# A graph attention whose aggregation products are issued in four parts between the K turns, one quad later

## The reference

```python
scores = jnp.einsum('ehd,ehd->eh', q[tgt], k[srcidx])        # 8 heads of 64
m = jax.ops.segment_max(scores, tgt, num_segments=n)
p = jnp.exp(scores - m[tgt])
s = jax.ops.segment_sum(p, tgt, num_segments=n)
w = p / (s[tgt] + 1e-16)
agg = jax.ops.segment_sum(w[:, :, None] * v[srcidx], tgt, num_segments=n)
```

## Time and profile before

| | us |
|---|---|
| median of 3 runs | 3487.64 (3484.23 to 3498.01) |
| the profiled execution | 3486.91 |
| its span | 3485.6 |
| PE busy | 2825.2 (81%) |
| POOL busy | 1161.3 (33%) |
| DVE, ACT busy | 1626.5, 1323.0 |
| attention of layer 0, steady part | 545 to 1380 of the span |
| attention of layer 1, steady part | 1960 to 2740 of the span |

### The profile page before, as it was taken

How to read it: one execution, slowest core, us unless ns; L and a number is a source line. 1 busy time by engine, 2 the same in 40 slices (tenths; PEclk the granted TensorE clock), 3 DMA queues, 4 the chain that set the end, 5 groups by cost and what they waited for, 6 DMA issues and landing times.

```text
span 3485.6 us, 78342 instructions
## 1 busy us (share of the span) xinstructions
PE 2825.2 (81%) x32605; PEld 2291.8 (66%) x32605; DVE 1626.5 (47%) x3272; ACT 1323.0 (38%) x3690; POOL 1161.3 (33%) x1130
## 2 busy tenths in 40 slices
PE   6999978888888888587996777777777758588888
PEld 5877866666676676464885666666666646366676
DVE  5247764444444444547123333333443455655443
ACT  3324434444444444322322344444444412243333
POOL 0000015555555555100012555655565401312110
PEclk8999989999999999789998899998988979799989
DMA  6531037887888888430234777777777642022211
GB/s 215 218 139 68 28 127 237 264 268 264 269 269 273 266 270 270 109 117 0 91 148 147 253 260 263 268 261 258 264 261 259 184 114 72 25 78 89 64 52 53
DMA packets 231795, 621.75 MB, mean 178 GB/s; under 512 B 39008, under 2 KB 45792, under 8 KB 231427
## 3 DMA queue, kind: packets, MB, share of 16 engines
q0 software_dynamic: 137088, 466.78, 40.1%
q1 hardware_dynamic: 94339, 149.78, 12.9%
HBM read 538.80 MB, written 103.39 MB: 184 GB/s over the span
## 4 chain that ended last, share of the span: by engine, by line
PE 75%; issue 12%; DVE 8%; DMA 2%; ACT 2%; another core or an unknown queue 1%; POOL 0%; SPq 0%; POOLq 0%; DVEq 0%; ACTq 0%
PE ps L1179 12%; PE ps L1221 9%; PE ps L1209 6%; PE ps L574 4%; PE ps L576 4%; PE ps L575 4%; PE ps L1186 3%; PE ps L774 3%; PE ps L942 2%; PE ps L944 2%; PE ps L943 2%; PE ps L1867 2%; PE ps L1171 1%; PE ps L1869 1%; PE ps L1868 1%
## 5 line engine op out<-in xcount | busy, mean ns | idle before, releaser
L1096 POOL DMA_INDIRECT Y<-KVd,srcE x449 | 457.2, 1018 | 374.9 <-PE ps L1221 237.8
L1277 DVE TENSOR_REDUCE stage<-ps 128x4 f32<-128x512 f32 x208 | 143.8, 692 | 629.8 <-remote 501.1
L1346 ACT ACTIVATE work<-ps 128x512 f32<-128x512 f32 x309 | 179.7, 597 | 506.8 <-PE ps L1179 472.3
L1221 PE MATMUL ps<-Y,G 128*32 128x64 f32 x7184 | 237.7, 226 | 161.9 <-issue 158.9
L1346 ACT ACTIVATE G<-ps 128x512 f32<-128x512 f32 x315 | 182.1, 598 | 421.8 <-PE ps L1179 388.4
L1096 POOL DMA_INDIRECT WA<-KVd,srcE x186 | 188.6, 1014 | 419.4 <-PE ps L576 266.3
L1221 PEld LDWEIGHTS ps<-Y,G 128*32 128x32 f32 x7184 | 181.9, 112 | 207.2 <-issue 202.7
L1365 ACT ACTIVATE stage<-ps,stage 128x128 f32<-128x128 f32 x832 | 294.0, 366 | 35.0 <-PE ps L1186 27.1
L1179 PE MATMUL ps<-ident,Y 128*128 128x128 f32 x1796 | 261.3, 303 | 2.6 <-issue 1.4
L574 PE MATMUL ps<-Wh,xs 128*128 128x512 f32 x600 | 239.0, 398 | 29.9 <-DVE xs L514 29.8
L1179 PEld LDWEIGHTS ps<-ident,Y 128*128 128x128 f32 x1796 | 231.9, 158 | 29.3 <-issue 21.0
(11 more groups left out here) (383 smaller groups left out, 6950.0 us busy)
## 6 DMA issues: line engine op xcount, KB each, us to landing
KVd<-stage SPq DMA_DIRECT2D x96, 256.0 KB, 2.0
aggd<-work SPq DMA_DIRECT2D x6, 2048.0 KB, 7.4
Qd<-stage SPq DMA_DIRECT2D x48, 256.0 KB, 2.0
G<-aggd SPq DMA_DIRECT2D x48, 256.0 KB, 2.7
Y<-KVd,srcE POOLq DMA_INDIRECT x449
Y<-in_x SPq DMA_DIRECT2D x4, 1536.0 KB, 15.0
G<-mixq SPq DMA_DIRECT2D x24, 256.0 KB
mixd<-rowsb SPq DMA_DIRECT2D x24, 256.0 KB
```

Source lines behind the costliest of these rows:

```text
L1096: pool.indirect_dma_start(out=kvs[a], out_offset=None, in_=KVd[l][:, :], in_offset=bass.IndirectOffsetOnAxis(ap=srcE[:, n:n + 1], axis=0)) ...
L1221: mm = pe.matmul(AG[32 * i:32 * i + 32, DH * h:DH * (h + 1)], probs[x][:, i, h, :], kvs[a][:, D + DH * h:D + DH * (h + 1)], start=(x == 0 ...
L1277: dve.tensor_reduce(smin[:, 4 * g:4 * g + 4], SC[g % 2][:, :].rearrange("p (c e) -> p c e", c=4), AXX, ALU.min).then_inc(mins, 1)
L1346: act.activation(kT[n % len(kT)], banks(l)[place_of(l, "k", n) % len(banks(l))][:, :], ACT.Copy).then_inc(out_a, 1)
```

## The change

Four things are altered.

1. In PE's round g the aggregation is that of quad g-3 (AGG_AT = 3), while the turn of the probabilities stays at quad g-2 (P_AT = 2).
2. `gather(g, i)` is one part: the eight products of tile i, all in column group i. Part 0 is issued after the second K turn of the round, parts 1 and 2 after the third and fourth, part 3 after the turn of the probabilities and ahead of the masks. The number of products is the same.
3. `agg` is raised once for each part, so by four in a quad; POOL's `fetch(n)` waits for the part of tile n-KV alone. All other waits on `agg` count by tiles.
4. In POOL's round the scatter stands ahead of the fetch of the queries. Because AGG_AT is odd now, both fall into the odd rounds; before, the scatter fell into even ones. On DVE the copy of the finished sums comes ahead of `least`. Each layer has one round more.

```diff
--- before.py
+++ after.py
@@ -27,7 +27,7 @@
 CAP = 16
 MASK = 2.0 ** 100
 LOOK = (2, 2)
-AGG_AT = 2
+P_AT, AGG_AT = 2, 3
 FAR = 8192.0
 BIG = 1.0e30
 EPS = 1e-5
@@ -835,8 +835,8 @@
                     order.append(("hot", b + 2))
                 if x == 1 and b + 1 < NJ:
                     order.append(("q", b + 1))
-                if g >= AGG_AT:
-                    order.append(("p", g - AGG_AT))
+                if 0 <= g - P_AT < NQ:
+                    order.append(("p", g - P_AT))
             place, by, count = {}, [], {"a": 0, "d": 0}
             for e, (kind, n) in enumerate(order):
                 who = "d" if kind in ("hot", "p") or kind == "k" and n % 4 == K_DVE[l] else "a"
@@ -1092,7 +1092,7 @@
             def fetch(n):
                 a = n % KV
                 if n >= KV:
-                    pool.wait_ge(agg, NQ * l + (n - KV) // 4 + 1)
+                    pool.wait_ge(agg, ET * l + n - KV + 1)
                 pool.indirect_dma_start(out=kvs[a], out_offset=None, in_=KVd[l][:, :],
                                         in_offset=bass.IndirectOffsetOnAxis(ap=srcE[:, n:n + 1], axis=0)
                                         ).then_inc(kv_in[a], 16)
@@ -1132,12 +1132,12 @@
                 fetch(n)
             at = KV
             for g in range(NQ + AGG_AT + 2):
+                x = (g - 2 - AGG_AT) // 2
+                if g % 2 == AGG_AT % 2 and 0 <= x < NJ:
+                    scatter(x)
                 j = (g + 3) // 2
                 if g % 2 and j < NJ:
                     fetch_slots(j)
-                x = (g - 2 - AGG_AT) // 2
-                if g % 2 == AGG_AT % 2 and 0 <= x < NJ:
-                    scatter(x)
                 while at < ET and (at - KV) // 4 <= g - AGG_AT:
                     fetch(at)
                     at += 1
@@ -1210,17 +1210,16 @@
                                    kT[n % len(kT)][:, k * P:(k + 1) * P], start=False, stop=True, skip_group_check=True)
                 mm.then_inc(sc, 1)
 
-            def gather(g):
-                x = g % 2
-                is_emptied(pe, l, place_of(l, "p", g))
-                if x == 0 and g:
-                    pe.wait_ge(ev, NJ * l + g // 2)
+            def gather(g, i):
+                x, a = g % 2, (4 * g + i) % KVN[l]
+                if i == 0:
+                    is_emptied(pe, l, place_of(l, "p", g))
+                    if x == 0 and g:
+                        pe.wait_ge(ev, NJ * l + g // 2)
                 for h in range(H):
-                    for i in range(4):
-                        a = (4 * g + i) % KVN[l]
-                        mm = pe.matmul(AG[32 * i:32 * i + 32, DH * h:DH * (h + 1)], probs[x][:, i, h, :],
-                                       kvs[a][:, D + DH * h:D + DH * (h + 1)], start=(x == 0 and h == 0), stop=(x == 1),
-                                       skip_group_check=True)
+                    mm = pe.matmul(AG[32 * i:32 * i + 32, DH * h:DH * (h + 1)], probs[x][:, i, h, :],
+                                   kvs[a][:, D + DH * h:D + DH * (h + 1)], start=(x == 0 and h == 0), stop=(x == 1),
+                                   skip_group_check=True)
                 mm.then_inc(agg, 1)
 
             if l == 0:
@@ -1239,21 +1238,23 @@
                 for i in range(4):
                     if 4 * g + LOOK[l] + i < ET:
                         turn_k(4 * g + LOOK[l] + i)
+                    if i >= 1 and g >= AGG_AT:
+                        gather(g - AGG_AT, i - 1)
                     if i == 1:
                         next(side, None)
                 if x == 0 and b + 2 < NJ:
                     turn_hot(b + 2)
                 if x == 1 and b + 1 < NJ:
                     turn_q(b + 1)
+                if 0 <= g - P_AT < NQ:
+                    turn_p(g - P_AT)
                 if g >= AGG_AT:
-                    turn_p(g - AGG_AT)
+                    gather(g - AGG_AT, 3)
                 next(side, None)
                 if g < NQ:
                     masks(g)
                     for i in range(4):
                         score(4 * g + i)
-                if g >= AGG_AT:
-                    gather(g - AGG_AT)
                 next(side, None)
 
         def attend_dve(l, side, begin, work_free):
@@ -1268,7 +1269,7 @@
                 x = g % 2
                 bank = bank_of("p", g)
                 if g >= 2:
-                    dve.wait_ge(agg, NQ * l + g - 1)
+                    dve.wait_ge(agg, ET * l + 4 * (g - 1))
                 dve.tensor_copy(probs[x][:, :, :, CAP * x:CAP * (x + 1)],
                                 bank[:, :].rearrange("p (c h s) -> p c h s", c=4, h=H)).then_inc(out_d, 1)
 
@@ -1291,7 +1292,7 @@
                 dve.tensor_tensor(p4, p4, rec4[:, :].unsqueeze(2).to_broadcast([P, 4, P]), ALU.mult).then_inc(normed, 1)
 
             def empty_agg(j):
-                dve.wait_ge(agg, NQ * l + 2 * j + 2)
+                dve.wait_ge(agg, ET * l + 4 * (2 * j + 2))
                 if j or l:
                     dve.wait_ge(sct, 16 * (NJ * l + j))
                 dve.tensor_copy(stage[:, 0, :], AG[:, :]).then_inc(ev, 1)
@@ -1321,15 +1322,15 @@
                 next(side, None)
                 if x == 0 and b + 2 < NJ:
                     empty_hot(l, b + 2)
-                if g >= AGG_AT:
-                    empty_p(g - AGG_AT)
+                if 0 <= g - P_AT < NQ:
+                    empty_p(g - P_AT)
                 next(side, None)
+                if g >= AGG_AT and (g - AGG_AT) % 2:
+                    empty_agg((g - AGG_AT) // 2)
                 if g < NQ:
                     least(g)
                 if 0 <= g - 1 < NQ:
                     normalise(g - 1)
-                if g >= AGG_AT and (g - AGG_AT) % 2:
-                    empty_agg((g - AGG_AT) // 2)
                 if x == 1 and b + 3 < NJ:
                     one_hot(l, b + 3)
                 next(side, None)
@@ -1387,7 +1388,7 @@
                 next(side, None)
 
         def edges_done(e, l):
-            e.wait_ge(agg, NQ * (l + 1))
+            e.wait_ge(agg, ET * (l + 1))
             e.wait_ge(ev, NJ * (l + 1))
 
         def edges_stored(e, l):
```

## The result

The changed kernel takes 4093.88 us (median of four runs, 4092.27 to 4096.43). The kernel before, beside it, takes 3492.82 (3484.23 to 3501.8). The ratio is 1.172, with a 95% interval of 1.169 to 1.176. That is 601 us more, where 367 were forecast; 4093.88 lies 4 us above the upper end of the range.

The account below looks back on a forecast made before the run. A ring between POOL's indirect-DMA chains and the PE stalls they cause was taken as the bound, with PE's work overtaking it after the change. Layer 1 +112, layer 0 +245 and extra rounds 10 made +367 on 3487: 3854 us, range 3530 to 4090.

Parts of the forecast that it names:

- The parts in series: Aggregation on PE: 16 matmuls of a part run in one column group, 0.88 us a part, 3.5 a quad against 0.9.
- Mode changes: PE between parts and full-array turns: ten changes a quad instead of two, 0.1 us each, +0.8 us, bounds 0 and 1.6.
- The stall: PE behind POOL's chain of five in odd rounds: 2.8 us a pair in layer 1, 2.3 in layer 0; even quads 0.5.
- The clock: PE's speed in both layers: the sum has no term for a lower clock; only rival C prices one.
- PE's own work: PE's time in a quad with no stall, after the change: 8.1 us in layer 1, 9.9 in layer 0.
- The sum's bases: Quad times of the kernel before, from which the additions are counted: 8.88 us in layer 0, 8.65 in layer 1.
- Moved waits: K turns waiting for K|V buffers held one round longer, layer 0: 0 to 1 us a pair, taken as 0.
- DVE's and the scatter's new places: DVE's copy of sums ahead of `least` and POOL's scatter ahead of the query fetch: both cost nothing.
- A: Rival, both layers: parts end the stalls, mode changes stay; +56 us, 3543; chance 0.18.
- D: Rival, both layers: POOL-PE ring broken, no stall left, mode changes hide; -133 us, 3354; chance 0.09.
- B: Rival, both layers: every round stalls in full, 2.3 us more in each even quad; +235 to the sum, 4089; chance 0.12.
- C: Rival, both layers: PE's clock falls to 1.2 GHz for half of the quads; +510 us, about 4360; chance 0.08.

Follow-up runs that it names:

- e1: Changed kernel with each of its four parts made of two heads of all four tiles, buffers released by quad: 3499.19 us, beside 3119.86 for the kernel before.
- e2: Kernel before, aggregation whole at its old place, with its tile loop outside the head loop: 3325.12 us, against 3119.86 unchanged.
- f1: Kernel before with K|V read by plain DMAs of SP (neighbouring rows) instead of POOL's indirect ones, chip with the stall: 3134.97 us against 3465.55.
- e6: Changed kernel with POOL's query fetch of odd rounds moved behind three K|V fetches, chip without the stall: 3608.38 us; kernel before 3137.59.
- r2: Changed kernel, unedited, on a chip without the stall: 3764.17 us against 3139.17 for the kernel before, ratio 1.200.

## Why the prediction was right in kind and too small

**The parts in series: right.** 55 ns a start and 0.88 us a part were forecast; 57 ns and 0.9 were measured. In layer 1, e1 against the kernel after shows that this order, and not the places, is the main cost. In layer 0 it isn't shown, since there the lateness holds e1 as well.

**Mode changes: right, a little small.** Of the pitch of 1.60 us, 16 x 57 ns = 0.91 and 4 x 109 ns = 0.44 are matmuls; 0.25 is left for two changes, 0.12 each, 0.1 in the forecast. e2 gives 0.12 as well. Without stalls and waits a quad is then 8.45 and 10.17 us, forecast 8.1 and 9.9: 0.35 and 0.27 too little, (0.35 + 0.27) x 102 = 63 us of the 234 missed.

**The stall: right in place and in size.** It stands where it was forecast, once in two rounds, behind the chain of five that starts at `turn_q`. In the even round its own fetches with their gaps cause none in the rows above. The pair of layer 1 that ran at the full clock throughout gives its size: 20.00 - 2 x 8.45 = 3.1 us, where 2.8 + 0.5 = 3.3 were forecast. Its first pause comes after some 50 matmuls and the idle that the profile lists after 59 (63 in the forecast), and it ends 1.16 us after the chain, not 0.3 to 0.9. f1 shows that the stall depends on the way in which K|V is fetched; that it is POOL's issuing stays an inference.

**The clock: the step that failed.** The sum counted PE's own work at 2.4 GHz throughout and had no term for what runs at 1.2 GHz behind a stall. Between 2505.13 and 2509.87 above PE takes 4.74 us for two parts and a K turn; at full clock these take 1.01 + 0.58 + 1.01 = 2.6. Not every pair loses as much: the three windows give 22.63 us at a mean clock of 0.85, 21.47 at 0.92, 20.00 at 1.00, and the mean of the layer, 21.8, lies 1.8 above the last. So the missing term is 1.8 us in a pair of layer 1. The forecast pair of 19.5, plus 0.7 of own work, less 0.2 of stall, plus 1.8 is the 21.8 measured.

The rows were there. The earlier trace rows shows turns at half speed behind a stall, and the earlier trace rows a mean of 0.90. I used them only for a rival that spread the lower clock over half of all quads. The mean clock of layer 1 is nearly the same before and after (0.89 in both windows above), so the low clock isn't new; what it costs is. Two neighbouring quads of the kernel before, from one chain of POOL to the next:

```profile
2310.12:2318.64 8.52, 5.97 (x126) 5.25 (x125) 2.84 (x6) 4.25 (x13) 5.12 (x5) 1.00 0.82 282
2318.64:2327.20 8.56, 7.14 (x123) 6.39 (x122) 3.95 (x9) 3.30 (x11) 5.11 (x6) 0.81 0.78 244
```

The second has its K turns at the lower clock and is only 0.04 us longer, because the turns ran beside POOL's chain, which set the length of a quad. In the changed kernel PE sets it, and every us lost to the clock counts.

In layer 0 a pair is 25.0 us, forecast 22.6. Of this 20.3 is PE's own (e6), so 4.7 are stall and lower clock together where 2.8 had been set. How they divide isn't measured. An estimate from the window's clock of 0.93: PE is at 1.2 GHz for 14% of 25.0 us, which costs at most half of that, 1.75, and leaves 3.0 or more for the stalls. The two layers' excess is (21.8 - 19.5)/2 x 102 = 117 and (25.0 - 22.6)/2 x 102 = 122. About 63 of it is own work, some 90 the clock in layer 1, and most of the rest, up to 89 by the estimate, the clock in layer 0. The sum's bases also differ by a few us from the later windows (8.88 and 8.65 against 8.94 and 8.57).

**Moved waits: 0 held here, but the reason given was wrong.** "It lands in time unless one more transfer is ahead; 0 to 1 us a pair, taken as 0, since PE then stalls anyway." On the chip with the stall layer 0 has only some 6 us of such waits in 1000. That is luck: without the stall they are 1.6 us a quad with the clock, 3.2 a pair, three times the upper bound. The working set "some 4 us" of slack against 1.95 us of transfer. In the rows of r2 above the data are there 4.5 us after POOL starts the fetch, and without the wait of 1.40 the turn would have come after 3.1. e6 starts the three fetches earlier, ahead of the wait for `turn_q`, and the waits go. Where the stall is, it gives the transfers the time that they lack.

**DVE's and the scatter's new places: nothing, as forecast.** In r2's layer 1 PE waits for nobody in 600 us.

**The rivals.** A (no stalls, 3543) and D (3354): false on the kind of chip that the forecast was for. The first half of A comes true on the others (no stall in r2), but the kernel before is then faster as well, so the change costs more, 627 us. B gave 4089, within 5 us of the result, by luck: its mechanism was a stall in full in every round, and in the rows the even rounds' fetches stall nothing. C (lower clock) has a true core, but only behind a stall, 1.8 us a pair and not 2.5 a quad; the mean clock of 0.91 is above the 0.85 that was to decide.

## What to carry to other kernels

Before cutting a packed aggregation into pieces, ask which loop is outermost inside a piece: pieces by column group run one group at a time (57 ns instead of 14 a matmul), pieces that keep all four groups in turn cost only the changes of mode. Price the work that will stand behind a stall at the clock that the rows behind stalls show, above all where the change makes PE the bound: a lower clock that cost 0.04 us a quad beside a longer chain cost 0.9 a quad once PE was the longer one. Hold the slack of a fetch against its measured time from issue to use (4.5 us here) and not against its transfer alone (1.95), waits ahead of it in its queue included. A gain on a bound that is not the same on every chip has to be measured on both kinds.

## What the hardware showed unexpectedly

- The same kernel takes 3465.55 us on one of the four numbered chips, 3493 on the chip of the two measurements, and 3120 to 3138 us on the three others. The difference goes away when SP fetches K|V with plain DMAs (3134.97). Each group of runs was of one kind throughout; whether the kind belongs to the chip or to something else on it isn't known.
- The stall starts some 50 to 63 matmuls, and as many weight loads, after POOL's chain of indirect DMAs does. The Trainium skill, TensorE: Matmul & The Clock Gate, Part 1, gives TensorE an engine queue of 64. That is near the count of matmuls but not of all instructions; that PE lives on what is in its queue while POOL issues is a guess, and no run here tests it.
- A change between the full array and column groups costs 0.12 us. The Trainium skill, TensorEngine Tiling (Array Packing), section Key Properties, says that such a change drains the engine; the trace agrees.
- Column groups in series overlap a little where one follows the other: 47 ns a start in one piece of 64, 57 in a part of 16.
